# First transformer layer taken one batch at a time, with 64-token expert matmuls and interleaved top-k rounds

## The chip, the core and the metric

The kernel runs on one core of one Trainium2 chip. TensorE (PE) multiplies, VectorE (DVE), ScalarE (ACT) and GpSimd (POOL) work on tiles in on-chip memory, and SyncE (SP) issues most of the transfers. The metric is the device time in microseconds of one execution. Every time below is measured on the chip.

## What is computed

Four batches of 256 tokens with 256 channels pass two gated layers. The reference, cut to its core:

```python
# layer 0: sparse adjacency from ctx, mixed with layernorm(x), then 4 fixed experts
sim = einsum('bhnd,bhmd->bnm', Q, K) / (sqrt(d) * H)          # ctx 4x256x64, H = 4
threshold = top_k(sim, 76)[0][:, :, -1:]
A = sigmoid(sim) * (sim >= threshold); A = (A + A^T) * 0.5
x = x + tanh(g_xattn[0]) * ((1 - gamma) * layernorm(x) + gamma * A)
x4 = layernorm(x).reshape(b, 64, 4, 256)                        # token n goes to expert n % 4
x = x + tanh(g_ffn[0]) * (silu(x4 @ gate) * (x4 @ up)) @ down
# layer 1: masked softmax of scores, then 64 experts, 8 for each token
x = x + tanh(g_xattn[1]) * softmax(scores(ctx) * layernorm(x) + mask)
p = softmax(layernorm(x) @ gate_w); rw = top 8 of p, normed
x = x + tanh(g_ffn[1]) * sum_e rw[:, e] * (silu(g_e) * u_e) @ w_down[e]
```

## The kernel before

Tokens are held as eight tiles of 128 rows, two to a batch. Everything is float32 but for a few counts. Each engine has one hand-written list of work; the lists meet only at semaphores, and each engine takes its list strictly in order. The program falls into three parts.

**The front part** computes layer 0, the attention of layer 1, and the router. Its steps for a batch `b` are these. `keep_top(b)` on DVE finds the 76th largest value of each row of `sim` in ten rounds; a round is two `max` (L991) and two `match_replace` (L995). `transpose_adj(b)` on PE (L573) and `mix_adjacencies(b)` on DVE (L1016, L1020) give the first sum. Each of three layernorms for a batch is `statistics` on DVE (L966 to L972), `inverse_deviation` on POOL (L439, L441), `normalise` on ACT (L827), `transpose_normed` on PE (L583) and `evacuate_xnt` on ACT (L832). The four experts of layer 0 are `expert_gate_up0` (L604) and `expert_down0` (L593) on PE, `silu_and_up0` on ACT (L847, L849) and `up_times_silu` on POOL (L449). They take 128 tokens an expert, out of two batches together, so there are eight calls `q`, four for each half of the batches. Then come `transpose_y0` (L615), `add_layer0` (L1025), `masked_scores`, `exp_scores` and `add_softmax`, `router_logits` on PE (L626), `choose_experts` (L1066 to L1072), `rank_rows` on PE (L672, L673) and DVE's `place_rows` (L1080 to L1092), which ends with `place_at`, the rows at which the batch's tokens are to be put for their experts.

**The placing** is POOL's `place_rows` (L478): 64 indirect transfers from `x_rows` to the DRAM buffer `expert_rows`, sixteen for each batch. The first of each batch waits for that batch's `place_at` and `x_rows`, and for `rows_cleared`, a transfer of 15 MB that fills the buffer with empty rows. SP issues it once, at L349. `inverse_deviation` of later layernorms stands between placements in POOL's list.

**The expert loop** runs over 63 of the 64 experts (and an overflow list). SP loads an expert's rows (L361) only when the placements of all four batches have landed (L360's wait on `placed[b]`); the loop on PE is L704, L715 and L724. Picks are scattered (L499), gathered and summed (L770).

PSUM has eight banks. The list `fills` gives every use of a bank a number in PE's order, and use `i` must wait (`begin(i)`) until use `i - 8` has been copied out. This is told by one semaphore for each copying engine, and `emptied` counts the uses of that engine:

```python
who = fills[i][1]
n = sum(1 for f in fills[:i + 1] if f[1] == who)
eng.wait_ge(evac[who], n)
```

Of the kernel before, what the change touches and what calls it, by code (L numbers as in the profile page):

```python
# [34 lines left out]
def gated_layers_kernel(nc, x, ctx_in, mask_ss, mask_bs, g_xattn, g_ffn, wq0, wk0, gamma_raw, gate_up, down,  # L35
# [12 lines left out]
    TE = HALF // NE0  # L48
# [17 lines left out]
    with ExitStack() as stack:  # L66
# [118 lines left out]
        evac = {who: sem(who + "_evac") for who in ("act", "dve")}  # L185
# [35 lines left out]
        F_CTX, F_PROJ, F_SIM, F_SCORE = {}, {}, {}, {}  # L221
        F_CTX[0] = add_fill("ctx", "act")
# [9 lines left out]
        for b in range(B):  # L232
            F_SCORE[b] = add_fill("score", "act")

        F_ADJT, F_XNT, F_YT, F_XNT2, F_LOGIT = {}, {}, {}, {}, {}
        F_GATE, F_UP, F_DOWN = {}, {}, {}

        def add_gate_up_fills(q):
            F_GATE[q], F_UP[q] = add_fill("gate", "act"), add_fill("up", "act")  # L240

        def add_down_fill(q):
            F_DOWN[q] = add_fill("down", "act")

        for fill, name, who in ((F_ADJT, "adjt", "dve"), (F_XNT, "xnt", "act")):
            for b in (0, 1):
                fill[b] = add_fill(name, who)
        for q in range(NE0):
            if q == NE0 - 1:
                F_ADJT[2] = add_fill("adjt", "dve")  # L250
            add_gate_up_fills(q)
            if q:
                add_down_fill(q - 1)
        add_down_fill(NE0 - 1)
        F_XNT[2] = add_fill("xnt", "act")
        F_ADJT[3] = add_fill("adjt", "dve")
        F_YT[0], F_YT[1] = add_fill("yt", "dve"), add_fill("yt", "dve")
        F_XNT[3] = add_fill("xnt", "act")
        add_gate_up_fills(NE0)
        for q in range(NE0 + 1, 2 * NE0 - 1):  # L260
            add_gate_up_fills(q)
            add_down_fill(q - 1)
        F_XNT2[0], F_XNT2[1] = add_fill("xnt2", "act"), add_fill("xnt2", "act")
        add_gate_up_fills(2 * NE0 - 1)
        F_LOGIT[0], F_LOGIT[1] = add_fill("logit", "act"), add_fill("logit", "act")
        add_down_fill(2 * NE0 - 2)
        add_down_fill(2 * NE0 - 1)
        F_RANK = {}
        F_RANK[0], F_RANK[1] = add_fill("rank", "dve"), add_fill("rank", "dve")
        F_YT[2], F_YT[3] = add_fill("yt", "dve"), add_fill("yt", "dve")  # L270
        F_XNT2[2], F_LOGIT[2] = add_fill("xnt2", "act"), add_fill("logit", "act")
        F_XNT2[3] = add_fill("xnt2", "act")
        F_RANK[2] = add_fill("rank", "dve")
        F_LOGIT[3] = add_fill("logit", "act")
        F_RANK[3] = add_fill("rank", "dve")
# [13 lines left out]
        LAYERNORMS = ((0, None), (1, 0), (1, 1), (1, 2), (1, 3), (2, 0), (2, 1), (3, 0), (3, 1), (2, 2), (2, 3), (3, 2), (3, 3))  # L289
# [11 lines left out]
        def xn_t_view(k, b, permuted):  # L301

            if permuted:
                return xn_t[:, k].rearrange("p (f e b g) -> p f e b g", f=2, e=NE0, b=B // 2)[:, b // 2, :, b % 2, :]
            return xn_t[:, k, b * S:(b + 1) * S]
# [99 lines left out]
        def _(pool):  # L405
# [37 lines left out]
            def up_times_silu(half, experts):  # L443
                for e in experts:
                    q = half * NE0 + e
                    emptied(pool, F_UP[q])
                    if q >= 2:
                        pool.wait_ge(bank_filled, F_DOWN[q - 2] + 1)
# [12 lines left out]
            for n, b in ((1, 2), (1, 3), (2, 0), (2, 1)):  # L461
                inverse_deviation(n, b)
# [28 lines left out]
            for b in range(1, B):  # L491
                place_rows(b, 0, PICKS)
# [784 lines left out]
```

## Time and profile before

| | |
|---|---|
| median of three runs | 417.0 us (415.72 to 417.07) |
| the profiled execution | 417.87 us |
| span of its trace | 416.1 us |
| first placement, last placement | 116.09, 200.86 us |
| first matmul of the expert loop | 206.52 us |

The trace's span leaves out 1.8 us that lie around it. A row of the lists view gives a line, an engine, an operation with output and inputs, the count and the summed and mean time. A row of the time view begins with the start and the duration in us, and ends with the idle time of the engine before it and what ended that.
### The profile page before, as it was taken

The numbers are of one execution on the slowest core, as the hardware profiler recorded it, in microseconds if no ns is written. First come the engines' busy times: TensorE is split into PE (matmuls) and PEld (weight loads), VectorE is DVE, ScalarE is ACT, GpSimd is POOL, SyncE is SP. The second block draws the span as 40 slices with busy tenths as digits, with TensorE's granted clock in tenths as the row PEclk, the third lists the DMA queues.
The fourth block names the chain that finished last, engine by engine and source line by source line (L and its number), as shares of the span: only waits on it lengthen the run. The fifth ranks groups of instructions, "written<-read, shape, count | busy, mean of one in ns | idle before, by whom it ended". The sixth has DMA issues, their size and how long they took to land.

```text
span 416.1 us, 5526 instructions
## 1 busy us (share of the span) xinstructions
PE 275.1 (66%) x1546; PEld 230.9 (55%) x1546; DVE 210.7 (51%) x921; ACT 118.0 (28%) x265; POOL 214.0 (51%) x256
## 2 busy tenths in 40 slices
PE   5898177137801610000199999999999999951997
PEld 1335067037800500000189999889999889931886
DVE  0799999989386679000033433343433343340352
ACT  2264353316634500000023333333333333320000
POOL 2622112013267777777327777777777777771000
PEclk9999999557975555555589999999999999995899
DMA  4899995360013333333498888888888887226891
GB/s 132 312 352 306 318 310 192 91 190 2 1 63 113 126 126 127 126 127 138 148 243 267 273 270 277 271 264 274 261 273 269 269 270 229 74 73 234 325 305 64
DMA packets 47374, 84.12 MB, mean 202 GB/s; under 512 B 10453, under 2 KB 28249, under 8 KB 46320
## 3 DMA queue, kind: packets, MB, share of 16 engines
q1 hardware_dynamic: 38128, 64.87, 49.9%
q0 software_dynamic: 9216, 18.90, 13.0%
q8 instruction: 13, 0.21, 0.2%
q14 instruction: 17, 0.14, 0.1%
HBM read 48.07 MB, written 39.85 MB: 211 GB/s over the span
## 4 chain that ended last, share of the span: by engine, by line
PE 52%; DVE 18%; POOL 16%; issue 7%; DMA 4%; ACT 2%; SPq 1%; POOLq 1%; ACTq 0%
PE psum L715 20%; POOL expert_rows L478 14%; PE psum L724 13%; PE psum L770 7%; PE psum L704 5%; DVE work L995 5%; DVE top L991 5%; DVE stats L966 2%; PE psum L536 2%; PE psum L530 2%; DMA sim<-token_picks 1%; POOL token_picks L499 1%; PE psum L604 1%; DVE adj L1000 1%; DMA gu_w<-expert_rows 1%
## 5 line engine op out<-in xcount | busy, mean ns | idle before, releaser
L499 POOL DMA_INDIRECT token_picks<-down_w,target x126 | 117.3, 931 | 54.9 <-issue 41.1
L715 PE MATMUL psum<-gu_w,wgu 128*96 128x192 f32 x504 | 93.7, 329 | 0.0
L715 PEld LDWEIGHTS psum<-gu_w,wgu 128*96 128x96 f32 x504 | 78.0, 165 | 0.6 <-DVE gu_w L1203 0.2
L478 POOL DMA_INDIRECT expert_rows<-x_rows,place_at x64 | 62.4, 975 | 23.8 <-issue 23.8
L724 PE MATMUL psum<-proj_t,gu_w 96*96 96x256 f32 x252 | 64.8, 379 | 0.0
L927 ACT ACTIVATE gu_w<-psum 96x192 f32<-96x192 f32 x63 | 20.6, 326 | 130.0 <-PE psum L715 130.0
L1208 DVE TENSOR_TENSOR gu_w<-gu_w,psum 96x192 f32<-96x192 f32 x63 | 22.1, 350 | 67.1 <-ACT gu_w L927 67.1
L704 PE MATMUL psum<-ident,gu_w 96*128 96x96 f32 x108 | 14.1, 256 | 53.1 <-DMA gu_w<-expert_rows 53.1
L933 ACT COPY down_w<-psum 96x512 f32<-96x512 f32 x63 | 36.6, 581 | 33.9 <-PE psum L724 33.9
L724 PEld LDWEIGHTS psum<-proj_t,gu_w 96*96 96x96 f32 x252 | 41.1, 163 | 7.1 <-DVE gu_w L1208 0.4
L704 PEld LDWEIGHTS psum<-ident,gu_w 96*128 96x128 f32 x108 | 12.5, 148 | 57.6 <-DMA gu_w<-expert_rows 54.4
L1203 DVE COPY gu_w<-psum 128x384 f32<-128x384 f32 x63 | 34.4, 547 | 0.0
L439 POOL TENSOR_TENSOR rstd<-var_eps,minus_half 128x2 f32<-128x2 f32 (+1 forms) x13 | 10.4, 797 | 46.6 <-DVE var_eps L972 46.5
L1202 DVE COPY target<-gu_w 96x2 uint32<-96x2 uint32 x27 | 4.5, 165 | 52.6 <-PE psum L704 52.6
L991 DVE MAX8 top<-work 128x8 f32<-128x256 f32 x72 | 26.8, 413 | 0.0
L995 DVE MATCH_REPLACE8 work<-top,work 128x256 f32<-128x256 f32 x64 | 25.7, 409 | 0.0
L604 PE MATMUL psum<-xn_t,gu_w 128*128 128x128 f32 x128 | 19.0, 316 | 1.7 <-ACT xn_t L832 1.7
L604 PEld LDWEIGHTS psum<-xn_t,gu_w 128*128 128x128 f32 x128 | 18.4, 231 | 2.4 <-issue 1.3
L449 POOL TENSOR_TENSOR h_t<-silu,up 128x256 f32<-128x256 f32 x8 | 6.1, 762 | 23.9 <-ACT up L849 23.6
L770 PE MATMUL psum<-sim,xn_t 128*128 128x256 f32 x32 | 9.9, 480 | 11.0 <-DMA sim<-token_picks 11.0
L1241 DVE TENSOR_TENSOR xs<-psum,scores 128x256 f32<-128x256 f32 x8 | 3.4, 424 | 27.3 <-PE psum L770 27.3
L583 PE MATMUL psum<-ident,x_rows 128*128 128x128 f32 x16 | 3.4, 351 | 20.8 <-ACT x_rows L827 19.8
(177 smaller groups left out, 397.1 us busy)
## 6 DMA issues: line engine op xcount, KB each, us to landing
expert_rows<-empty_rows SPq DMA_DIRECT2D x1, 15360.0 KB, 69.3
wgu<-in_L_ffn_w_gate_up SPq DMA_DIRECT2D x65, 192.0 KB, 2.9
gu_w<-expert_rows SPq DMA_DIRECT2D x28, 240.0 KB, 4.2
proj_t<-in_L_ffn_w_down SPq DMA_DIRECT2D x65, 96.0 KB, 4.0
sim<-expert_rows SPq DMA_DIRECT2D x18, 240.0 KB, 4.3
work<-expert_rows SPq DMA_DIRECT2D x18, 240.0 KB, 4.2
gu_w<-in_L_ffn_gate_up_proj SPq DMA_DIRECT2D x4, 512.0 KB, 8.2
sim<-token_picks SPq DMA_DIRECT2D x2, 1024.0 KB, 4.9
```

The lines of the kernel that those rows point to most:

```text
L478: pool.indirect_dma_start(rows_dram, bass.IndirectOffsetOnAxis(ap=place_at[:, t, k:k + 1], axis=0), x_rows[:, t, :], None).then_inc(placed ...
L499: pool.indirect_dma_start(picks_dram, bass.IndirectOffsetOnAxis(ap=target[0:SLOTS, e % T_RING, i:i + 1], axis=0), y_slots[0:SLOTS, n, i, : ...
L604: last = pe.matmul(bank(fill)[:, ic * TE:(ic + 1) * TE], gu_w[:, e, k, c:c + P], xn_t[:, k, half * HALF + e * TE:half * HALF + (e + 1) * T ...
L704: last = pe.transpose(psum[:, e % 2, k * CAP + i * SLOTS:k * CAP + (i + 1) * SLOTS], x_slots[n][0:SLOTS, i, k * P:(k + 1) * P], ident[0:SL ...
L715: last = pe.matmul(psum[0:I1, 2 + e % 2, part * CAP:(part + 1) * CAP], wgu[:, n, k, part * I1:(part + 1) * I1], x_slots_t[:, e % 2, k, :], ...
L724: last = pe.matmul(psum[0:SLOTS, 4 + e % 2, i * D:(i + 1) * D], h1_t[:, e % 2, i * SLOTS:(i + 1) * SLOTS], wd[:, n, :], start=True, stop=True)
L770: last = pe.matmul(psum[:, t, 0:D], diag[:, t % 2, k, :], picks[t % K_RING][:, k * D:(k + 1) * D], start=k == 0, stop=k == TOP_K_EXPERTS - 1)
L933: act.copy(y_slots[0:SLOTS, n].rearrange("p i d -> p (i d)"), psum[0:SLOTS, 4 + e % 2, 0:SUBS * D]).then_inc(y_ready, 1)
L991: dve.max(top8[:, t, r], (work if r else sim)[:, t]).then_inc(top8_ready, 1)
L995: dve.match_replace(work[:, t], top8[:, t, r], (work if r else sim)[:, t], REMOVED).then_inc(rest_ready, 1)
L1203: dve.tensor_copy(x_slots_t[:, e % 2].rearrange("p k n -> p (k n)"), psum[:, e % 2, 0:KC * CAP]).then_inc(xt_copied, 1)
L1208: dve.tensor_tensor(h1_t[:, e % 2], silu1[:, e % 2], psum[0:I1, 2 + e % 2, CAP:2 * CAP], ALU.mult).then_inc(h_ready, 1)
```

## The change

The front part is written in another order, and four things in it are of another shape.

1. The four experts of layer 0 take one batch at a time: 64 tokens an expert, sixteen calls `q`. Gate and up share a bank, and four `down` results share one, which ACT empties with two copies. The number of matmuls doubles, each on half the columns.
2. For batches 2 and 3 the product of silu and up moves from POOL to DVE, which reads `up` out of PSUM. ACT then copies no `up`.
3. `keep_top` is cut into pieces of one to ten rounds, and these stand between the layernorm, softmax and router steps of earlier batches.
4. Every kind of bank use has its own semaphore, so ACT and DVE may empty banks in another order than PE fills them. POOL's four groups of sixteen placements stand in batch order as before, but the later layernorms are spread over the first three groups.

SP's list is the same. Its eight weight loads still wait until the last `scores` has been copied, which now comes after batch 0's experts.

The diff, cut:

```diff
-    TE = HALF // NE0
+    TE = S // NE0
...
+        evac = {who: sem(who + "_evac") for who in ("act", "dve", "score", "adjt", "xnt", "yt", "xnt2", "logit", "rank", "gu", "gu_dve", "down")}
+        down_step, silu0_ready = sem("down_step"), sem("silu0_ready")
...
+                  ("gu", 4), ("gu", 5), ("gu", 6), ("gu", 7), ("down", 1),
+                  ("xnt2", 0), ("logit", 0), ("yt", 1), ("adjt", 2), ("rank", 0), ("xnt", 2),
+                  ("gu_dve", 8), ("gu_dve", 9), ("gu_dve", 10), ("gu_dve", 11), ("down", 2),
...
+            def expert_gate_up0(q):
+                b, e = q // NE0, q % NE0
+                begin(F_GU[q])
+                for part in range(2):
                     for ic in range(IC):
                         for k in range(KC):
+                            c, at = part * I0 + ic * P, (part * IC + ic) * TE
+                            last = pe.matmul(bank(F_GU[q])[:, at:at + TE], gu_w[:, e, k, c:c + P],
+                                             xn_t[:, k, b * S + e * TE:b * S + (e + 1) * TE], start=k == 0, stop=k == KC - 1)
+                last.then_inc(bank_filled, 1)
...
+            def evacuate_down(b):
+                filled(F_DOWN[b])
+                for k in range(KC):
+                    last = act.copy(y0_t[:, k, b * S:(b + 1) * S].rearrange("p (n e) -> p e n", e=NE0),
+                                    bank(F_DOWN[b]).rearrange("p (e k n) -> p k e n", k=KC, e=NE0)[:, k])
+                last.then_inc(evac["down"], 1)
...
+            def up_times_silu(*which):
+                for q in which:
+                    dve.wait_ge(silu0_ready, q - 2 * NE0 + 1)
+                    dve.wait_ge(down_step, q - 1)
+                    dve.tensor_tensor(h0_t[:, q % 2].rearrange("p i t -> p (i t)"), silu0[:, q % 2], bank(F_GU[q])[:, IC * TE:2 * IC * TE],
+                                      ALU.mult).then_inc(h0_ready, 1)
```

Three places show the order. A row is a line, an operation with output and inputs, and the output's shape. **PE, experts of layer 0.** Before, the first half of the batches, with the transposes of `adj` for batches 0 and 1 ahead and that for batch 2 in between:

```order
L573 MATMUL psum<-ident,adj 128x128 x8
L583 MATMUL psum<-ident,xn 128x128 x8
L604 MATMUL psum<-xn_t,gu_w 128x128 x16
L593 MATMUL psum<-h_t,down_w 128x128 x4
L604 MATMUL psum<-xn_t,gu_w 128x128 x8
L593 MATMUL psum<-h_t,down_w 128x128 x4
L573 MATMUL psum<-ident,adj 128x128 x4
L604 MATMUL psum<-xn_t,gu_w 128x128 x8
L593 MATMUL psum<-h_t,down_w 128x128 x8
```

After, batch 1 alone, up to its router and the rank of batch 0:

```order
L557 MATMUL psum<-ident,xn 128x128 x4
L584 MATMUL psum<-xn_t,gu_w 128x64 x16
L570 MATMUL psum<-h_t,down_w 128x64 x4
L584 MATMUL psum<-xn_t,gu_w 128x64 x8
L570 MATMUL psum<-h_t,down_w 128x64 x4
L584 MATMUL psum<-xn_t,gu_w 128x64 x8
L570 MATMUL psum<-h_t,down_w 128x64 x8
L557 MATMUL psum<-ident,x_rows 128x128 x4
L606 MATMUL psum<-router,xn_t 128x64 x4
```

One batch now has as many expert matmuls (48) as two batches together had, and its router follows at once. **POOL, placements.** Before, from the first placement on:

```order
L478 DMA expert_rows<-x_rows,place_at 65728x320 x2
L439 TENSOR_TENSOR rstd<-var_eps,minus_half 128x2
L441 TENSOR_TENSOR shift<-neg_mean,rstd 128x2
L478 DMA expert_rows<-x_rows,place_at 65728x320 x2
...
L478 DMA expert_rows<-x_rows,place_at 65728x320 x6
...
L478 DMA expert_rows<-x_rows,place_at 65728x320 x3
...
L478 DMA expert_rows<-x_rows,place_at 65728x320 x51
```

After, with the same pair of layernorm rows at each "...":

```order
L448 DMA expert_rows<-x_rows,place_at 65728x320 x2
L414 TENSOR_TENSOR rstd<-var_eps,minus_half 128x2
L416 TENSOR_TENSOR shift<-neg_mean,rstd 128x2
L448 DMA expert_rows<-x_rows,place_at 65728x320 x7
...
L448 DMA expert_rows<-x_rows,place_at 65728x320 x10
...
L448 DMA expert_rows<-x_rows,place_at 65728x320 x5
...
L448 DMA expert_rows<-x_rows,place_at 65728x320 x9
...
L448 DMA expert_rows<-x_rows,place_at 65728x320 x6
...
L448 DMA expert_rows<-x_rows,place_at 65728x320 x23
```

Seven layernorm pairs stand among the placements now, four did before, and the last stands 23 placements from the end. **DVE, around the first batch's choice.** Before, what follows the last statistics of batch 1:

```order
L1066 MAX l_top<-logits 128x8 x2
L1068 TENSOR_SCALAR l_neg<-l_top 128x2
L1070 MATCH_REPLACE logits_left<-l_top,logits 128x64 x2
L1072 TENSOR_SCALAR chosen<-logits_left 128x128
...
L1080 SCALAR_TENSOR_TENSOR order<-chosen,zeros 128x64 x2
```

After, batch 0's choice comes behind the last round of batch 2, and ahead of the whole search of batch 3:

```order
L1011 MAX top<-work 128x8 x2
L1022 SCALAR_TENSOR_TENSOR adj<-sim,top,adj 128x256 x2
L1099 MAX l_top<-logits 128x8 x2
L1101 TENSOR_SCALAR l_neg<-l_top 128x2
L1103 MATCH_REPLACE logits_left<-l_top,logits 128x64 x2
L1105 TENSOR_SCALAR chosen<-logits_left 128x128
L1038 TENSOR_TENSOR adj<-adj,psum 128x512
L1042 SCALAR_TENSOR_TENSOR xs<-adj,coef,base 128x512
```

All four searches stood ahead of the first choice before.

## Rows read from the trace of the kernel before

**Rows 1.** The page's chain that ended last, by line
```profile
PE psum L715 20%; POOL expert_rows L478 14%; PE psum L724 13%; PE psum L770 7%; PE psum L704 5%; DVE work L995 5%; DVE top L991 5%; DVE stats L966 2%; PE psum L536 2%; PE psum L530 2%; DMA sim<-token_picks 1%; POOL token_picks L499 1%; PE psum L604 1%; DVE adj L1000 1%; DMA gu_w<-expert_rows 1%
```
**Rows 2.** Time view, POOL: first placement, two around a layernorm pair, last ones
```profile
116.09 1.23 POOL L478 DMA_INDIRECT expert_rows<-x_rows,place_at  x1 [5.18 <-issue]
...
121.68 1.02 POOL L478 DMA_INDIRECT expert_rows<-x_rows,place_at  x1 [0.30 <-issue]
...
123.91 1.04 POOL L478 DMA_INDIRECT expert_rows<-x_rows,place_at  x1 [0.16 <-issue]
...
142.46 0.96 POOL L478 DMA_INDIRECT expert_rows<-x_rows,place_at  x1 [0.30 <-issue]
...
200.86 0.96 POOL L478 DMA_INDIRECT expert_rows<-x_rows,place_at  x1 [0.30 <-issue]
```
**Rows 3.** Chain in order of time (start, us, what): the expert loop begins
```profile
206.52 1.72 PE psum L704 x8
```
**Rows 4.** Time view, DVE: the places of batch 3
```profile
146.90 0.39 DVE L1092 TENSOR_SCALAR place_at<-place 128x16 uint32<-128x16 f32 x1
```
**Rows 5.** Chain in order of time: one round of the search on DVE
```profile
54.32 0.65 DVE top L991 x2
54.97 0.79 DVE work L995 x2
```
**Rows 6.** The clearing: the page's DMA issues (KB, us to landing), then its issue
```profile
expert_rows<-empty_rows SPq DMA_DIRECT2D x1, 15360.0 KB, 69.3
...
16.19 0.61 SPq L349 DMA_DIRECT2D expert_rows<-empty_rows  x1
```
**Rows 7.** Stretches, PE's L604 (128 columns), then L626 (64), L770 (256)
```profile
94.06:98.06 4.00, 4.00 (x19) 0.50 0.02 6
...
135.50:137.20 1.70, 1.70 (x8) 0.50 0.47 172
109.53:111.27 1.74, 1.74 (x16) 1.00 0.00 0
...
390.00:398.00 8.00, 8.00 (x38) 1.00 0.88 279
```
**Rows 8.** Chain in order of time: sixteen records of L604 at the full clock
```profile
107.91 1.79 PE psum L604 x16
```
**Rows 9.** Stretches, all of PE, before and at changes of the granted clock
```profile
32.70:39.70 7.00, 7.00 (x16) 1.00 1.00 308
...
97.00:98.00 1.00, 1.00 (x6) 0.50 0.00 0
98.00:99.00 1.00, 1.00 (x10) 0.90 0.00 0
...
383.00:388.00 5.00, 4.97 (x12) 0.50 1.01 426
```
**Rows 10.** Time view, DVE: layer 0 added with its statistics, and masked scores
```profile
117.00 0.75 DVE L1025 SCALAR_TENSOR_TENSOR xs<-psum,tg,xs 128x512 f32<-128x512 f32 x1
...
118.93 0.16 DVE L972 TENSOR_SCALAR var_eps<-mv 128x2 f32<-128x2 f32 x1
...
121.00 0.88 DVE L1034 SCALAR_TENSOR_TENSOR work<-xs,mv,scores 128x256 f32<-128x256 f32 x2
...
122.72 0.24 DVE L1042 SCALAR_TENSOR_TENSOR exp_bias<-row_max,rstd 128x1 f32<-128x1 f32 x2
```
**Rows 11.** Time view: batch 2 from its last statistics to its router
```profile
132.23 0.20 DVE L972 TENSOR_SCALAR var_eps<-mv 128x2 f32<-128x2 f32 x1
...
132.44 1.09 ACT L827 ACTIVATE x_rows<-xs,shift,rstd 128x256 f32<-128x256 f32 x2 [4.09 <-POOL shift L441]
134.80 0.65 ACT L832 COPY xn_t<-psum 128x256 f32<-128x256 f32 x2 [1.27 <-PE psum L583]
...
133.68 1.08 PE L583 MATMUL psum<-ident,x_rows 128*128 128x128 f32 x4 [18.61 <-ACT x_rows L827]
135.50 1.97 PE L626 MATMUL psum<-router,xn_t 128*128 128x64 f32 x8 [0.74 <-ACT xn_t L832]
```

More of the change, by code:

```diff
@@ L248, in gated_layers_kernel @@
[L248 to L262, printed above, removed]
@@ L563, in _ @@
                     emptied(pe, F_PROJ[w, half])
-            for b in range(B):
-                query_times_key(1, F_SCORE, b)
             def transpose_adj(b):
@@ L859, in copy_logits @@
                 filled(F_LOGIT[b])
[L860 removed]
+                act.copy(logits[:, span(b)].rearrange("p h n -> p (h n)"), bank(F_LOGIT[b])[:, 0:HB * NE]).then_inc(evac["logit"], 1)
             def exp_logits(b):
@@ new lines, in _ @@
+            sigmoids(1)
+            scale_x(0)
+            copy_scaled(scores, F_SCORE, 0, SCORE_SCALE)
+            copy_scaled(scores, F_SCORE, 1, SCORE_SCALE)
+            normalise(1, 0)
+            evacuate_xnt(F_XNT, True, 0)
+            sigmoids(2)
+            sigmoids(3)
+            act.preload_act_table(ACT.Silu)
+            copy_scaled(scores, F_SCORE, 2, SCORE_SCALE)
+            scale_x(1)
+            silu_and_up0(0, 1, 2, 3)
+            normalise(1, 1)
+            evacuate_down(0)
@@ L882, in _ @@
+            copy_scaled(scores, F_SCORE, 3, SCORE_SCALE)
+            evacuate_xnt(F_XNT, True, 1)
+            silu_and_up0(4, 5)
             act.preload_act_table(ACT.Exp)
-            for b in (2, 3):
-                normalise(1, b)
-                evacuate_xnt(F_XNT, True, b)
             exp_scores(0)
+            act.preload_act_table(ACT.Silu)
+            silu_and_up0(6, 7)
+            scale_x(2)
+            evacuate_down(1)
+            normalise(3, 0)
+            evacuate_xnt(F_XNT2, False, 0)
@@ L980, in _, with keep_top @@
                               ALU.mult).then_inc(evac["dve"], 1)
-            def keep_top(b):
+            def keep_top(b, first, end):
                 emptied(dve, F_SIM[b])
                 tiles = range(b * HB, (b + 1) * HB)
-                for r in range(ROUNDS):
+                for r in range(first, end):
                     for t in tiles:
@@ L1125, in _ @@
+            up_times_silu(8)
+            keep_top(3, 1, 2)
+            up_times_silu(9)
+            softmax_and_statistics(1)
+            keep_top(3, 2, 3)
+            up_times_silu(10)
+            keep_top(3, 3, 4)
+            up_times_silu(11)
+            keep_top(3, 4, 6)
+            choose_experts(1)
+            keep_top(3, 6, 7)
+            place_rows(1)
+            keep_top(3, 7, ROUNDS)
+            add_layer0(2)
             mix_adjacencies(3)
             statistics(1, 3)
-            for b in (0, 1):
-                add_layer0(b)
-                statistics(2, b)
```

376 lines of the change are left out of this document (198 added, 178 removed).

## The prediction

> **What bounds the kernel now.** I read the chain that ended last first [rows 1]: most of it is PE's loop over the experts (L704, L715, L724) and the last sums (L770), and 14% is POOL's placing (L478). Next POOL in time: the first placement starts at 116.09, the last at 200.86, and from 142.46 on it goes 46 steps without a gap [rows 2]: (200.86 - 142.46) / 46 = 1.27 us each. The loop begins at 206.52 [rows 3], 5.66 after the last placement starts: landing, and SP's load of the first rows. Batch 3's places were ready at about 147.3 [rows 4], long before POOL reached them. So DVE's front part ends 35 us too early to matter at its end; what decides is when POOL may start and whether it ever waits. From 206.52 to the span's end is 209.6 us, in which nothing changes. The whole sum is therefore one number: **when does the last placement start?** It has two bounds. POOL: first placement plus 64 x 1.27, plus layernorm pairs at 2.23 - 1.27 = 0.96 each [rows 2]. Data: the last batch's places plus 15 x 1.27 = 19.1.
>
> **The change, part by part.**
>
> *What moves earlier.* Batch 0's choice now comes after three searches, not four, and without batch 1's steps. A round of the search takes 0.65 + 0.79 = 1.44 [rows 5], a search about 14.6, ten rounds. On the other side the clearing of the row buffer lands at 16.19 + 69.3 = 85.5 [rows 6], and before that nothing may be placed. SP's order is unchanged, so I keep 85.5. If everything else were ready, the first placement would gain 116.1 - 85.5 = 30.6 us, and three more pairs cost 2.9 of that: a gain of at most 27.7.
>
> *What it costs on PE.* The matmuls of layer 0's experts double in number at half the columns. Is a 64-column matmul cheaper? At the lower clock a record of 128 columns (L604) takes 4.00 / 19 = 0.21, and one of 64 columns (the router, L626) 1.70 / 8 = 0.2125 [rows 7]; at the full clock 1.79 / 16 = 0.112 [rows 8] and 1.74 / 16 = 0.109. Both come with a 128x128 weight load. So halving the columns saves nothing, and a batch's 48 matmuls are 96 records: **20.4 us at the lower clock, 10.5 at the full one**. Before, two batches together paid that.
>
> *Which clock.* This decides the sign. The granted column says 1.00 for 32.70 to 39.70, but sixteen records of 256 columns took 7.00 there, 0.44 each, in matmuls of 64 rows [rows 9]; the last sums, 128 rows and also 256 columns, take 8.00 / 38 = 0.21 at the full clock [rows 7] and 4.97 / 12 = 0.41 at 0.50 [rows 9]. So the early stretch really ran at 1.2 GHz, and an unbroken run of half-height matmuls did not change that. What PE did before it rose to 2.4 GHz was each time a stretch of full-height matmuls of 128 columns (98 us) or 256 (after 388 us) [rows 7, 9]. After the change no such stretch is left ahead of the expert loop: scores are half height, expert matmuls half as wide, the rest is transposes and routers. The full-clock row with 64 columns [rows 7] follows at once on 128-column matmuls, so it shows that the clock can stay, not that it would rise. I take 1.2 GHz for the whole front part.
> The Trainium skill speaks against this: "TensorE: Matmul & The Clock Gate", Part 1, says that activity over time releases the throttle, whatever the number of matmuls; by that rule each batch's long run would reach 2.4 GHz, and the sum would be that of the first rival below. The half-height run does not agree with it. The same page, Part 4, adds that transposes do not count as activity, which no row here tests alone.
>
> *Layout and small terms.* DVE gets eight products of 128x128 from PSUM, under 0.5 each: two 128x256 steps take 0.88 together (L1034) [rows 10]; POOL loses eight of 0.7. Bank semaphores by class cost nothing by themselves. Four more table loads on ACT stand nearly all where ACT waits for PE.
>
> *The sum at 1.2 GHz.* I laid the five lists beside each other, every step starting when its engine and its inputs are free. The same laying of the old lists gives 116.7 for the first and 201.6 for the last placement, against 116.1 and 200.9, so I compare with 201.6. Landmarks:
> - Batch 0 is normalised at 41, its experts run from 43.6 to 65.1 (20.4, and batch 1's transposes of `adj` in between). Then scores 3 (two matmuls of 256 columns, 1.9), two times four transposes (0.9 each), ACT's copy 0.7: batch 1's experts run from 69.7 to 90.3.
> - The router of batch 0 is *behind* batch 1's experts on PE. From 90.3: copies and layernorm 1.8, transposes 1.1, copy 0.65, router 1.97 [rows 11], copy: DVE gets logits at 96.1 and has by then waited for them, and for transposes before. Choice 1.2, mix and statistics of batch 2 2.8, places 2.1: first placement at **102.4**, 17 after the clearing, 14 earlier than before.
> - Batch 2's experts from 104.5 to 125.2, its clock-bound path again before batch 1's router; places of batch 1 at **133.8**. POOL has finished group 0 at 127.3 and waits.
> - The last three rounds of batch 3's search (4.3), layer 0 of batch 2, mix, statistics: 142.2. Batch 3's experts start at 146.3; with router and transposes between, the ranks of batch 2 come at 168.9, its places at **170.1**. POOL had ended group 1 at 161.6 and waits 8.5.
> - Layer 0 of batch 3 is added at 172.5, statistics and masked scores follow with 2.0 and 1.9 [rows 10], softmax and statistics to 181.7. The layernorm pair stands behind nine placements of group 2 and starts at 183.2. From there as in [rows 11]: 1.0, 1.1, 1.1, 0.65, 1.97, with hops and a copy 189.4; choice and places 3.6: **193.0**, exactly when POOL has done group 2 (170.1 + 16 placements + two pairs + 0.7 of waiting).
> - Last placement at 193.0 + 19.0 = 212.0, against 201.6: **+10.4 us**. From the profiled 417.87: 428.3. That execution lay 0.9 above the median, so I predict **427.5**.
> Bounds: at 0.205 a record the last placement is at 209.3, at 0.23 (a record's price if starts after waits cost more) at 218.7, so 424.5 to 434; I take 0.2125, the 64-column row itself.
>
> **Rivals.**
> 1. *The clock rises in each batch's run*, as for 128 columns. The same laying with 0.11 a record once a run has lasted as long as the one at 94 us needed: experts of batch 0 from 43.5 to 56.4, of batch 1 60.1 to 71.8; places of batch 0 at 82.2. Now the clearing binds: first placement 85.5, and DVE waits 3.3 for a layernorm that stands behind two placements. Places of batches 1, 2 and 3 at 108.8, 139.2 and 161.3, POOL free at 161.4: last placement at 180.3, **-21.3**, that is 395.7. For it: PE would be busy for more than 10 us on end. Against: [rows 9] as read above.
> 2. *The clock rises in some of the four runs only.* The two layings differ by 31.7, about 8 a batch: 404, 412 or 420.
> 3. *The clearing lands later*, held up by nothing now but perhaps by the weight loads' new time: at 95 instead of 85.5 the fast case loses 9.5 (405), the slow case nothing.
> 4. *The placing stays where it was*, because the data bound of batch 3 cancels what the start gains: the two meet if a record costs 0.183, between the two prices; then 417. It needs a clock that changes midway.
>
> **How the numbers follow.** Slow clock throughout: 0.57, 424.5 to 434. Rival 1: 0.32, 393 to 400. Rivals 2 and 3: 0.09, nearly all of it faster. Rival 4: 0.02. A measurement tells 0.3% (1.3 us) from no change. Faster 0.40, same 0.02, slower 0.58. No range on one side holds 8 in 10, so it runs from 394 to 433; the likeliest case's own is 424.5 to 434.
>
> **What would show it.** Right: granted clock 0.50 (or 64-column records at 0.21) from the first expert matmul to past the placing; first placement near 102; POOL waiting before groups 1 and 2, 6 and 8 us; DVE idle for logits; last placement near 211; loop start 5.7 later, and 209.6 from there. Wrong on the clock: records at 0.11 and first placement at 85.5. Wrong on the price: records clearly under 0.21 at 0.50, so that halving the columns did save. Wrong on the tail: anything but 209.6 after the loop's start.

## The result, and the profile after

The changed kernel takes **430.81 us** (430.04 to 432.85, 4 runs), the kernel before, beside it on the same chip, 416.72 us (415.72 to 417.07). The ratio is 1.035, with a 95% interval of 1.0308 to 1.0392: 14.1 us slower. The forecast was 427.5, with 424.5 to 434 for its own case and 394 to 433 over all cases.

First the page, its chain by line and two lines of the busy tenths (40 slices of 10.7 us):

```profile
PE psum L719 19%; PE psum L728 13%; PE psum L584 11%; POOL expert_rows L448 7%; PE psum L774 7%; PE psum L570 6%; PE psum L708 5%; DVE work L1015 3%; DVE top L1011 2%; PE psum L557 2%; PE psum L513 1%; DVE stats L987 1%; PE psum L606 1%; DMA sim<-token_picks 1%; POOL rstd L414 1%
...
PE   4896999974993399222039999999999999980997
POOL 2713011013772572677714777777777777772000
```

Before, layer 0's expert matmuls (L604) were 1% of this chain and the placing 14% [rows 1]. Now L584 and L570, the same work in 64-column pieces, are 17%, and the placing is 7%: half of POOL's share has gone, and PE's experts have taken its place.

POOL in time shows the same with its waits. The columns are start, duration, engine, line, operation, tiles, and in brackets the idle time ahead of it:

```profile
104.29 1.23 POOL L448 DMA_INDIRECT expert_rows<-x_rows,place_at  x1 [1.76 <-issue]
...
136.17 0.96 POOL L448 DMA_INDIRECT expert_rows<-x_rows,place_at  x1 [7.65 <-issue]
...
144.10 0.72 POOL L414 TENSOR_TENSOR rstd<-var_eps,minus_half 128x2 f32<-128x2 f32 x1 [4.45 <-DVE var_eps L993]
...
172.83 0.96 POOL L448 DMA_INDIRECT expert_rows<-x_rows,place_at  x1 [9.25 <-issue]
...
196.54 0.96 POOL L448 DMA_INDIRECT expert_rows<-x_rows,place_at  x1 [0.94 <-issue]
...
215.88 0.96 POOL L448 DMA_INDIRECT expert_rows<-x_rows,place_at  x1 [0.30 <-issue]
```

The first placement starts 11.8 us earlier than in [rows 2] (104.29 against 116.09), and the last one 15.0 us later (215.88 against 200.86). In between POOL waits 7.65, 4.45 and 9.25 us for the next batch's data; before, it went 46 steps without a gap. The loop over the experts follows at 221.43, 5.55 after the last placement, and the rest of the span is 428.3 - 221.43 = 206.9.

Why the data come late is seen on PE. Time view of PE, the first batch's experts, then stretches (duration, PE busy, number of records, granted clock, DMA share, GB/s):

```profile
43.77 7.09 PE L584 MATMUL psum<-xn_t,gu_w 128*128 128x64 f32 x32
50.65 1.92 PE L570 MATMUL psum<-h_t,down_w 128*128 128x64 f32 x8
...
70.09:77.09 7.00, 7.00 (x32) 1.00 0.30 84
...
221.43:225.27 3.84, 3.84 (x15) 1.00 0.97 268
225.27:227.00 1.73, 1.73 (x15) 1.00 1.06 278
...
389.10:399.35 10.25, 3.07 (x7) 0.50 0.72 273
```

32 records take 7.00 us, 0.219 each. That is the price of the lower level, 1.2 GHz, as [rows 7] have it for 64 columns, and not the 0.109 of the full clock. The granted column nevertheless reads 1.00, as it did in [rows 9] for a stretch that ran at the lower level: in these traces the column shows no level below 1.00 until the clock falls for the first time, so ahead of that the records' own durations have to be read. By them the first rise lies at 225.27, 3.84 us into the loop over the experts: 15 records take 3.84 us up to there and the next 15 take 1.73. Ahead of it no run of matmuls in the front part is faster than the lower level, where the kernel before reached the full level in both of its expert runs.

### The profile page after: what moved, and what is told of

It is laid out like the page before. It is cut to its first block, busy times and chain, and to the rows that moved or that the text cites. A ratio compares the mean times of both kernels' runs of the same rounds, so it can differ in the third digit from the quotient of the medians.

```text
span 428.3 us, 5963 instructions
## 1 busy us (share of the span) xinstructions
PE 335.4 (78%) x1738; PEld 289.9 (68%) x1738; DVE 214.1 (50%) x929; ACT 123.0 (29%) x269; POOL 209.5 (49%) x256
## 4 chain that ended last, share of the span: by engine, by line
PE 69%; DVE 10%; POOL 9%; issue 4%; DMA 3%; ACT 2%; SPq 1%; POOLq 0%; PEldq 0%; DVEq 0%; ACTq 0%
PE psum L719 19%; PE psum L728 13%; PE psum L584 11%; POOL expert_rows L448 7%; PE psum L774 7%; PE psum L570 6%; PE psum L708 5%; DVE work L1015 3%; DVE top L1011 2%; PE psum L557 2%; PE psum L513 1%; DVE stats L987 1%; PE psum L606 1%; DMA sim<-token_picks 1%; POOL rstd L414 1%
## 5 line engine op out<-in xcount | busy, mean ns | idle before, releaser
L476 POOL DMA_INDIRECT token_picks<-down_w,target x126 | 115.4, 916 | 54.5 <-issue 41.1
L584 PE MATMUL psum<-xn_t,gu_w 128*128 128x64 f32 x256 | 57.1, 421 | 2.2 <-ACT xn_t L831 2.2
L584 PEld LDWEIGHTS psum<-xn_t,gu_w 128*128 128x128 f32 x256 | 55.9, 332 | 4.1 <-ACT xn_t L831 3.4
L570 PE MATMUL psum<-h_t,down_w 128*128 128x64 f32 x128 | 30.1, 422 | 0.0
L414 POOL TENSOR_TENSOR rstd<-var_eps,minus_half 128x2 f32<-128x2 f32 (+1 forms) x13 | 10.4, 797 | 38.8 <-DVE var_eps L993 38.6
L570 PEld LDWEIGHTS psum<-h_t,down_w 128*128 128x128 f32 x128 | 28.8, 333 | 0.0
L422 POOL TENSOR_TENSOR h_t<-silu,up 128x128 f32<-128x128 f32 x8 | 3.6, 453 | 36.5 <-ACT up L847 36.5
L845 ACT ACTIVATE silu<-psum 128x128 f32<-128x128 f32 x16 | 4.4, 277 | 46.0 <-PE psum L584 46.0
L557 PE MATMUL psum<-ident,x_rows 128*128 128x128 f32 x16 | 4.4, 428 | 15.9 <-ACT x_rows L826 15.6
```

The source lines that it names most:

```text
L476: pool.indirect_dma_start(picks_dram, bass.IndirectOffsetOnAxis(ap=target[0:SLOTS, e % T_RING, i:i + 1], axis=0), y_slots[0:SLOTS, n, i, : ...
L570: last = pe.matmul(bank(i)[:, c:c + TE], down_w[:, e, ic, hc * P:(hc + 1) * P], h0_t[:, q % 2, ic, :], start=ic == 0, stop=ic == IC - 1)
L584: last = pe.matmul(bank(F_GU[q])[:, at:at + TE], gu_w[:, e, k, c:c + P], xn_t[:, k, b * S + e * TE:b * S + (e + 1) * TE], start=k == 0, st ...
```

## The experiments

Each was timed beside the kernel before. For e1 to e8 that one took 416.7 to 417.1 us; for e9 to e12 it took 477 to 478, of which more below. "Last placement" is the start of the last of POOL's 64 placements, the one number of the prediction's sum. A matmul with f32 operands shows as two records.

### Is it the clock, and what decides it?

**e3_old_split**, the old order with the new matmuls:

```
-  for k in range(KC):
-      last = pe.matmul(bank(fill)[:, ic*TE:(ic+1)*TE], gu_w[...], xn_t[..., 128 columns])
+  for g in (0, TE // 2):
+      for k in range(KC):
+          last = pe.matmul(bank(fill)[:, ic*TE+g:ic*TE+g+64], gu_w[...], xn_t[..., 64 columns from g])
   (the down matmuls likewise)
```

> Edit: the kernel before, in its own order, with each expert matmul of layer 0 (128 columns) issued as two of 64 columns into the two halves of the same region: twice as many matmuls, as in the change, and nothing else changed. Theory: no clock rise ahead of the expert loop any more, records at 0.2135 throughout; the five lists laid beside each other give the last placement 46.6 us later (two batches' 192 records stand in one run, twice), so 463 us (450 to 468). Rival A in the form that doubling alone costs and the clock rises as before: 8.4 us more, 425 us.

Measured: 460.34 us (459.72 to 460.92), ratio 1.1054 (1.1035 to 1.1072). One stretch of all of PE, and POOL's last placement:

```profile
57.23:98.88 41.65, 41.65 (x196) 1.00 0.49 152
...
245.66 0.96 POOL L478 DMA_INDIRECT expert_rows<-x_rows,place_at  x1 [0.30 <-issue]
```

PE is busy for 41.65 us without a gap, in full-height matmuls (192 records of 64 columns and four transposes), and 196 records take 0.2125 each: the lower level from end to end (the 1.00 is again the column ahead of the first fall). In the three executions that were not profiled the column's mean is 0.825 to 0.829 instead of 0.989, at the same time within 1.2 us; their traces were not kept, and it is one more reason not to read the level from that column. So here being busy didn't raise the clock, and neither did full height alone. The Trainium skill, "TensorE: Matmul & The Clock Gate", Part 1, has sustained activity release the throttle; taken as "PE busy", that rule doesn't hold for this row.

**e5_old_twice**, as many matmuls, but 128 columns each:

```
-  for k in range(KC):
+  for k in list(range(KC)) * 2:
       last = pe.matmul(... 128 columns ..., start=k == 0, stop=k == KC - 1)
   (the down matmuls likewise)
```

> Edit: the kernel before, in its own order, with each expert matmul of layer 0 issued twice at its full 128 columns (the second contraction writes over the first), so as many matmul instructions as e3_old_split, and 128 columns instead of 64. The pair tells the number of matmuls from the clock. Theory (columns decide the clock): it rises about 4 us into each run as in the kernel before, records at 0.11 from there, last placement 11.5 us later than before: 428 us (425 to 434). Rival A (number of matmuls is the price): as e3_old_split, 460 us.

Measured: 430.24 us (430.06 to 431.08), ratio 1.0309. PE's first expert run, then the last placement:

```profile
57.01 9.72 PE L604 MATMUL psum<-xn_t,gu_w 128*128 128x128 f32 x64 [0.93 <-ACT xn_t L832]
...
68.35 3.74 PE L604 MATMUL psum<-xn_t,gu_w 128*128 128x128 f32 x32
...
214.11 0.96 POOL L478 DMA_INDIRECT expert_rows<-x_rows,place_at  x1 [0.30 <-issue]
```

64 records in 9.72 us, then 32 in 3.74 (0.117 each): the clock rose in the first run. e3 and e5 have the same order and the same number of matmuls; they differ by **30.1 us**, and by 31.55 in the last placement, and that is the columns, through the clock. Rival A, that the number is the price whatever is streamed, falls. What number alone costs is e5 less the kernel before, 13.1 us against the one timed beside it (417.12) and 13.5 against 416.72.

**e1_wide**, the changed kernel with 128-column gate/up matmuls:

```
-  last = pe.matmul(bank(F_GU[q])[:, at:at + TE], gu_w[...], xn_t[:, k, own 64 columns])
+  last = pe.matmul(bank(F_GU[q])[:, at:at + 2*TE], gu_w[...], xn_t[:, k, the pair's 128 columns])
   (ACT and DVE read the expert's own half of each 128)
```

> Theory (the front part stays at 1.2 GHz because no stretch of full-height matmuls of 128 or more columns is left in it). Edit: in the changed kernel each gate/up matmul of layer 0's experts streams the 128 columns of an expert pair instead of its own 64; ACT and DVE read only the expert's own half of the bank. Same number of matmuls, same order, same results; only 8 of 12 matmuls of an expert are wider. The theory expects the clock to rise within about 4 us of batch 0's first expert matmul, records at 0.11 from there, first placement at the clearing's landing, about 85.5, last placement near 180: 215.88 of the changed kernel minus 35.6, so 395 us (range 393 to 401). Rival A (the number of matmuls is the price, whatever they stream): nothing changes in records at 0.2135, last placement 215.9, 431 us. Rival B (the order of the lists, with routers and layernorms behind experts and placements, holds the placing back): first placement stays above 100 though the clock rises; 415 to 425 us.

Measured: **405.67 us** (404.25 to 407.45), ratio 0.9751 (0.9711 to 0.9791): streaming twice the columns, half of which nobody reads, makes the changed kernel 25.1 us faster, and faster than the kernel before by 11.0. The gate/up run at the head of batches 0 to 3, then POOL's groups:

```profile
43.75 5.10 PE L592 MATMUL psum<-xn_t,gu_w 128*128 128x128 f32 x32
...
60.72 3.84 PE L592 MATMUL psum<-xn_t,gu_w 128*128 128x128 f32 x32 [0.74 <-ACT xn_t L839]
...
86.94 5.67 PE L592 MATMUL psum<-xn_t,gu_w 128*128 128x128 f32 x32 [0.74 <-ACT xn_t L839]
...
125.94 6.60 PE L592 MATMUL psum<-xn_t,gu_w 128*128 128x128 f32 x32 [0.74 <-ACT xn_t L839]
...
85.59 1.24 POOL L455 DMA_INDIRECT expert_rows<-x_rows,place_at  x1 [1.75 <-issue]
113.93 0.95 POOL L455 DMA_INDIRECT expert_rows<-x_rows,place_at  x1 [5.52 <-issue]
146.34 0.96 POOL L455 DMA_INDIRECT expert_rows<-x_rows,place_at  x1 [5.03 <-issue]
188.61 0.96 POOL L455 DMA_INDIRECT expert_rows<-x_rows,place_at  x1 [0.30 <-issue]
```

The first placement is where the theory had it, 85.59, though not by the clearing alone: that landed at 83.9, and DVE wrote the places at 84.6. The last came 8.6 us later than its 180, and the 405.67 us lie outside the 393 to 401 that were expected: batch 1 enters its experts at the full level (3.84 for 32 records), but batches 2 and 3 pay 5.67 and 6.60. The clock had fallen earlier, in or right behind a wait of PE of 2.26 us (at about 73.7, ahead of the transposes of x_rows, and at about 101.1), and in the 5.0 and 5.3 us of idle time ahead of the experts nothing raised it. The expectation had let it stay up. Rival B, that the lists' order holds the placing at 100 or more, falls.

**e4_half**, half of the matmuls at the lower clock:

```
-  for k in range(KC):  ... start=k == 0, stop=k == KC - 1
+  for k in range(1):   ... start=True, stop=True
   (ic in the down matmuls likewise)
```

> Edit: the changed kernel with half of layer 0's expert matmuls left out (one half of each contraction, k = 0 and ic = 0 alone), so 48 records of 64 columns a batch; the output differs by what they would add. Theory: clock still low (64 columns), but the records' time halves to 10.2 a batch; last placement 183.9 in the laying, so 399 us (395 to 405). If order (rival B) were the limit: 415 or more. If the clock rises here: 394, which the records' duration (0.21 or 0.11) tells apart.

Measured: 401.5 us (400.19 to 403.23). PE's first expert run, and POOL's first and last placement:

```profile
43.77 3.67 PE L584 MATMUL psum<-xn_t,gu_w 128*128 128x64 f32 x16
...
85.29 1.23 POOL L448 DMA_INDIRECT expert_rows<-x_rows,place_at  x1 [1.76 <-DMA expert_rows<-empty_rows]
...
184.94 0.96 POOL L448 DMA_INDIRECT expert_rows<-x_rows,place_at  x1 [0.31 <-issue]
```

16 records in 3.67: the lower clock, half the records, and the kernel is 29.3 us faster than the changed one. PE's time in layer 0's experts falls by 4 x 10.2 = 40.8 us and the last placement comes 30.9 earlier, so three quarters of that time were on the path that ends last. e1 saves about as much by the clock (27.3 at the last placement) as e4 by number. The clearing landed at 84.3 here and DVE wrote the places at 84.3 too; below 85.3 little is to be had at that end.

### Can the clock be raised from outside?

**e2_burst**: 24 dummy matmuls ahead of each batch's experts.

```
+  def keep_busy(q, times):
+      begin(F_GU[q])
+      for _ in range(times):
+          pe.matmul(bank(F_GU[q])[:, 0:P], ident[:], ctx_rows[:, 0:2, :], start=True, stop=True)
+  keep_busy(0, 24)                      (and 4, 8, 12 ahead of the later batches)
   emptied(pe, F_XNT[0])
   expert_gate_up0(0)
```

> Edit: in the changed kernel 24 matmuls of 128x128 by 128 columns, f32 and full height, that write over a bank about to be filled, stand ahead of each batch's expert matmuls of layer 0; the experts stay at 64 columns. Results unchanged. Question: can the clock be raised from outside, and does a run of 64-column matmuls hold it? If it rises in each burst and is held: a burst costs 4.4 us at the lower clock, the records behind it 0.11; first placement 88, last 187, so 402 us. If it rises and falls again within the run: between, 425 to 445 us. If it never rises: each burst is 5 us of delay on the way of its batch, last placement at 234, 449 us.

Measured: 423.99 us (419.5 to 425.19), ratio 1.0141.

```profile
43.88 7.32 PE L626 MATMUL psum<-ctx_rows,ident 128*128 128x128 f32 x48
51.03 3.68 PE L584 MATMUL psum<-xn_t,gu_w 128*128 128x64 f32 x32
...
72.57 3.68 PE L584 MATMUL psum<-xn_t,gu_w 128*128 128x64 f32 x32
```

I had priced the burst wrongly, as 24 records; it is 48, and took 7.32, 6.20, 7.62 and 8.01 us in the four batches, each on the path: 29.2 us instead of 17.6. That is only part of the miss of 22 us against the 402 of a held clock; the last placement came at 206.09 instead of 187, and in batch 2 the level was lost again in a wait of 2.26 us for `h0`. But one answer is clear: the 64-column records behind the burst cost 0.115 to 0.12, in all of batches 0 and 1. Matmuls that had not raised the clock ran at it, and four bursts that compute nothing make the kernel 6.8 us faster than the changed one.

**e8_narrow_idle** put such dummies only where PE stood idle anyway:

```
+  keep_busy(F_XNT[2], 11)
   transpose_normed(F_XNT, xn, xn_ready, 2)
+  keep_busy(F_XNT[3], 12)
   transpose_normed(F_XNT, xn, xn_ready, 3)
```

> Edit: the changed kernel with its 64-column expert matmuls, and only the fill of PE's idle time ahead of the transposes of xn of batches 2 and 3 (11 and 12 dummy matmuls of 128 columns). Theory: 64-column matmuls can't raise the clock but hold it, as they did for a whole batch behind each burst of e2_burst. Then batches 0 and 1 stay at 0.21 a record, batches 2 and 3 run at 0.11 throughout: first placement unchanged at 104.3, last at 200 instead of 215.9: 415 us (412 to 421). If the clock does not rise in the idle fill or is lost at once: 431 to 432.

Measured: 428.5 us (428.26 to 430.4): 2.3 below the changed kernel instead of 16. PE in batch 2:

```profile
98.60 3.72 PE L626 MATMUL psum<-ctx_rows,ident 128*128 128x128 f32 x22
103.75 0.63 PE L557 MATMUL psum<-ident,xn 128*128 128x128 f32 x4 [1.43 <-ACT xn L833]
105.12 4.88 PE L584 MATMUL psum<-xn_t,gu_w 128*128 128x64 f32 x32 [0.74 <-ACT xn_t L838]
...
111.67 3.62 PE L584 MATMUL psum<-xn_t,gu_w 128*128 128x64 f32 x16
```

The fill did raise the clock (four transposes in 0.63 instead of 1.09), and it was lost inside the first 32 expert records (4.88), back to 3.62 for 16. The expectation that 64 columns hold the clock was wrong here, though in e2 they had held it for whole batches. In batch 3 of this trace they held it through their first 32 records (3.79), and it fell in the 3.60 us in which PE then waited for `h0`.

**e6_wide_idle** is e1 with the same two fills:

> Edit: e1_wide, and in the idle time of PE ahead of the transposes of xn of batches 2 and 3 (5.0 and 5.3 us idle there in e1_wide) 11 and 12 dummy matmuls of 128x128 by 128 columns (22 and 24 records, 4.9 and 5.3 us at 1.2 GHz) into the bank that these transposes then fill. Theory: PE's own idle time lets the clock fall, and e1_wide enters the experts of batches 2 and 3 at 0.50; with the idle time filled they run at 0.11 a record from the first, places of batches 1, 2 and 3 come 4.5, 6.3 and 6.3 us earlier, last placement near 182.3: 399.5 us (397 to 403). Rival: the clock does not rise in so short a fill, or falls again in the 0.7 us ahead of the experts: 405.7 as e1_wide, or up to 1 us more.

Measured: 405.88 us (401.58 to 406.95), the rival's time and not the theory's 399.5, but not by the rival's cause. PE in batches 2 and 3, and two stretches of PE there:

```profile
88.78 3.84 PE L592 MATMUL psum<-xn_t,gu_w 128*128 128x128 f32 x32 [0.74 <-ACT xn_t L846]
...
126.05 3.84 PE L592 MATMUL psum<-xn_t,gu_w 128*128 128x128 f32 x32 [0.74 <-ACT xn_t L846]
133.42 1.94 PE L577 MATMUL psum<-h_t,down_w 128*128 128x64 f32 x8 [3.54 <-DVE h_t L1071]
...
129.90:133.42 3.52, 0.00 (x0) 0.97 0.39 141
133.42:140.10 6.68, 6.44 (x30) 0.50 0.31 112
```

Both fills worked: 32 records in 3.84 at the head of both batches. But batch 3's down matmuls wait 3.54 for `h0` from DVE, whose multiplication stands behind the softmax and statistics of batch 2; what PE gained it waits out, and in that wait the clock falls to 0.50 again. Besides, batch 1's run had already lost the clock in this execution (first placement 87.89 instead of 85.59), with a program that up to there is that of e1: 128-column matmuls lose it at times too.

**e7_wide_idle_pool** moves three of POOL's layernorm pairs: (2, batch 2) and (3, batch 3) one placement earlier each, and (3, batch 2) two. (In the changed kernel's list of placements under "The change", two placements stand between the ten and the five, with one more pair: the groups are 2, 7, 10, 2, 5, 9, 6 and 23, 64 in all with seven pairs.)

> Edit: e6_wide_idle, and on POOL the layernorm pair of (2, batch 2) one placement earlier, the one of (3, batch 3) one earlier. What is left of the order's price: DVE waits 3.2 us for the pair (2, 2) behind placements in e1_wide. Laying the lists gives 1.3 us less than e6_wide_idle: 398 us (396 to 402). Rival: the placing is bound elsewhere and nothing changes (within 0.5 us of e6_wide_idle).

Measured: **402.87 us** (398.38 to 404.72), ratio 0.962 (0.9569 to 0.9671), the fastest of all, but outside the 396 to 402 expected, and neither the theory's 1.3 below e6_wide_idle nor the rival's nothing. The last placements of the two profiled executions, 189.14 and 189.64, lie only 0.5 apart, and the loops start 0.7 apart. Another 1.6 of the 2.4 us between these two executions lies behind the loop's start, where nothing in the program differs. So what moving the pairs is worth is not shown beyond half a microsecond, and in e1's trace, without any fill, the last placement lay at 188.61.

### What stays open: the other idle time, and the old order

**e9_wide_filled**, **e12_filled_again** (the same kernel) and **e10_narrow_filled** fill nearly all idle time around the experts:

```
   expert_gate_up0(13)
+  keep_busy(F_XNT2[2], 14)
   expert_down0(12)
   ...
+  keep_busy(F_GU[4], 3)                 (and ahead of y0's transposes, and in batch 2)
   emptied(pe, F_XNT[1])
```

> Edit: e7_wide_idle_pool with the rest of PE's idle time around the experts filled by dummy matmuls too: 3 ahead of the transposes of y0, 3 in each wait for ACT's copy of xn (0.74 us), 7 and 3 among batch 2's last experts (waits of 1.6 and 0.8 us in e6_wide_idle), 14 ahead of batch 3's first down matmuls (3.5 us there, in which the clock fell to 0.50 again). Theory: in e6_wide_idle the gain went because PE's waits for h0 let the clock fall within the batches; filled, it stays at 1.00 from batch 2's transposes to its router, and through batch 3's experts; places of batch 2 at about 138 instead of 147.6, last placement near 181: 397 us (394 to 401). Rival: the clock isn't what holds batch 2's places back, but DVE's and ACT's lists; 402 to 404 as e7_wide_idle_pool.

> Edit: the same fills, the changed POOL order and 10 dummies ahead of batch 0's experts, but the experts at the changed kernel's own 64 columns. Two runs stand against each other: behind the long bursts of e2_burst 64-column matmuls ran at 0.11 for whole batches, in e8_narrow_idle the clock fell 2.7 us into batch 2's. If 64 columns hold the clock once no idle time is left: as e9_wide_filled within 2 us. If they don't hold it behind a short fill: it falls within each batch, records at 0.21 from there, first placement at 92 to 100, 410 to 428 us.

> Edit: none against e9_wide_filled, the same kernel once more. There the kernel before took 477 us instead of 417 (its expert loop was longer), and in batch 2 of the filled kernel ACT stood 5.5 us in a wait put down to nothing on this core, so e9 does not tell whether the fills help. Where the kernel before takes 417: group 1's places then come about 5.5 us earlier than the 119.2 of e9, the last placement at 184 to 188 instead of 196.8; against 189.1 of e7_wide_idle_pool that is 400 us (396 to 403) if the held clock is worth anything beyond e7; if it is not, 402 to 404 as e7.

Measured: 465.6 us (e9), 467.53 (e10) and 467.76 (e12), where the kernel before took 477.4 beside the first two and 477.93 beside the third: ratios 0.9749 (0.9702 to 0.9795), 0.9761 (0.9713 to 0.9809) and 0.9836 (0.9782 to 0.989). On these chips engines stood still at many places for a few us with no releaser on this core, in the loop above all, which took 218.6 us in e9 and 164.8 in e7. One such row, ACT in batch 2 of e9; then PE's granted clock from batch 2's fill on:

```profile
102.12 0.28 ACT L867 ACTIVATE silu<-psum 128x128 f32<-128x128 f32 x1 [5.51 <-remote]
...
84.00:98.00 14.00, 11.96 (x101) 1.00 0.69 223
129.40:137.00 7.60, 7.53 (x65) 1.00 0.30 109
137.00:146.00 9.00, 8.40 (x75) 1.00 0.29 106
```

The fills do most of what they are for: batch 3's experts run at 1.00 up to their last down matmuls (1.97 for 8 records, behind waits of 2.3 and 1.5 us). In batch 2 the level fell at about 100.7 all the same. Whether that beats e7 is **not settled**: such stops put group 1's places of e9 at 119.21 against 115.8 in e7, and e12 met the same conditions instead of answering. Against the kernel before beside them e9 and e12 gain 11.8 and 10.2 us, e7 14.3. e10 says something about 64 columns all the same:

```profile
48.27:70.00 21.73, 21.30 (x178) 1.00 0.86 287
86.00:96.00 10.00, 8.09 (x68) 0.99 0.54 177
98.00:104.00 6.00, 6.00 (x30) 0.50 0.30 109
```

Behind ten dummies 178 records, about 150 of them of 64 columns, ran through batches 0 and 1 in 21.30 us (0.12 each) with the clock held; in batch 2 it was lost some 2 us after a wait of 1 us for `h0`; in batch 3 it held again. The time, 1.9 us above e9's, lies within the 2 us that were expected for a held clock, so the time doesn't tell the two cases apart. So 64-column matmuls hold the clock sometimes (e2, e10 in batches 0, 1 and 3) and sometimes not (e8 and e10 in batch 2). Both losses came soon after PE had stood idle for about a microsecond or more. With 128 columns batch 2 kept the clock behind the very wait at which e10 lost it (0.98 us in e6, 0.97 in e9), which points at the columns; but e6 lost it in its batch 1 behind waits of 0.9 and 0.7 us. With one trace of each this stays an observation.

**e11_old_idle** gives the kernel before the same care:

> Edit: the kernel before, in its own order and with its own matmuls, with PE's idle time ahead of both expert runs of layer 0 filled with dummy matmuls (9, 4 and 3 ahead of the first, 7 and 3 ahead of the second). Question: is the gain of the filled versions the clock alone, or the new order that the clock makes worth having? Expected from the laying: the experts of both halves start at 1.00 and save 2 us each, but the first placement waits for DVE's four searches, so 416 us (413 to 417.5). If the clock alone were the gain: 405 or less.

Measured: 479.22 us (474.12 to 481.12), ratio 1.0024 (0.9992 to 1.0055).

```profile
56.60 3.81 PE L604 MATMUL psum<-xn_t,gu_w 128*128 128x128 f32 x32 [0.27 <-ACT xn_t L842]
...
118.17 1.23 POOL L478 DMA_INDIRECT expert_rows<-x_rows,place_at  x1 [5.17 <-issue]
```

The expert run starts at the full level, and the first placement is no earlier than in [rows 2]. In the old order the clock isn't worth having sooner: the ratio leaves room for 0.1% at most. That DVE's four searches are what holds it back is the reading that the expectation started from, and the unmoved first placement agrees with it.

## Why the prediction was right, and where it was off

**The three parts of the 14.1 us**, each from a pair of runs:

| step | from | to | us |
|---|---|---|---|
| twice the matmuls, clock still rises | before, 416.7 | e5, 430.2 | +13.5 |
| 64 columns, clock never rises | e5, 430.2 | e3, 460.3 | +30.1 |
| the new order and all else of the change | e3, 460.3 | after, 430.8 | -29.5 |

The new order is worth 29.5 us at the same matmuls and the same clock; the way in which it cuts the matmuls costs 43.6. With a clock that rises the order is worth 24.6: e5, 430.24, against e1, 405.67, which have the same number of matmuls (e1's down matmuls have 64 columns).

**Which clock: right, and it decided the sign.** The prediction read from [rows 9] that a busy half-height stretch had not raised the clock, and concluded that with the 128-column stretches gone nothing would. No rise came before 225.27. The row that it argued from was of another shape (64 rows, 256 columns), so the step to full-height matmuls of 64 columns was a leap, given 0.57; e3 is what bears it out. Its list of the rises left one out: in the kernel before the clock also rose at 210.8, 4.3 us into the loop, behind matmuls of 96 and 192 columns (L704, L715), and the same place is the first rise of the changed kernel. Rival 1, whose time was 395.7, is what e1 would have been had the clock also stayed up between batches; its laying gave first placement 85.5 (e1: 85.59) and last placement 180.3 (188.61).

**The price of a record: right.** Batch 0's experts were laid from 43.6 to 65.1 and lay from 43.77 to 65.3; batch 1's 69.7 to 90.3, measured 70.09 to 90.8. Halving the columns saved nothing.

**The landmarks: right in order, late by a growing bit.** First placement 102.4 laid, 104.29 measured; POOL's wait ahead of group 1 about 6, measured 7.65; ahead of group 2 8.5, measured 9.25; batch 3's experts 146.3 against 148.19; the third pair of batch 3 183.2 against 185.81; the last group 193.0 against 196.54; last placement 212.0 against 215.88. **The step that was mis-sized is the handing over from engine to engine.** DVE's writes of the places of batches 0 and 3, to set beside POOL's starts at 104.29 and 196.54:

```profile
103.17 0.17 DVE L1125 TENSOR_SCALAR place_at<-place 128x16 uint32<-128x16 f32 x1
...
195.59 0.17 DVE L1125 TENSOR_SCALAR place_at<-place 128x16 uint32<-128x16 f32 x1
```

The last placement is 3.9 late, in three pieces. The places of batch 3 end at 195.76 where 193.0 was laid: 2.8 had piled up ahead of POOL. PE's expert runs themselves took what was laid (21.5, 20.7 and 20.7 us for batches 0 to 2), so it lies between them; one piece that can be named is the layernorm behind batch 1's experts, 2.2 us of waiting on PE where 1.8 was laid. POOL then starts 0.8 after the write, 0.95 in batch 0, and the landmarks had nothing for that, as if places ready meant placement started. The last fifteen placements took 19.34 instead of 19.0. The laying of the old lists, by which I corrected, was late by 0.7, so a constant correction taken from it had the wrong sign. Together it makes 4.6 us: +15.0 instead of +10.4.

**The tail: wrong by 2.7**, in the other direction: 206.9 behind the loop's first matmul instead of 209.6. Nothing in the code differs there. The first matmuls of the last sums, before and after:

```profile
383.03 6.31 PE L770 MATMUL psum<-sim,xn_t 128*128 128x256 f32 x16 [11.04 <-DMA sim<-token_picks]
...
396.28 5.21 PE L774 MATMUL psum<-sim,xn_t 128*128 128x256 f32 x16 [10.18 <-DMA sim<-token_picks]
```

Of the 2.7, 0.9 is the wait for the gathered picks, 1.1 are these 16 records, of which fewer ran at the lower level, and 0.8 lies in the loop, at whose start the lower level lasted 3.84 us instead of 4.3. "Nothing changes from there" held for the instructions and not for the transfers and the clock. Nor is it peculiar to the change: in the profiled executions of e1 to e8 the same stretch took 206.8 to 211.8 us. A tail taken from one execution carries an error of that size, and that it went the helpful way is luck.

The two misses have opposite signs, 4.6 and 2.7, so the profiled execution came out only 1.7 above the 428.3 forecast for it. The other 1.6 of the 3.3 between the medians is where the profiled executions lie: 0.9 above the median before, 0.8 below it after. So the nearness of the forecast owes something to errors that cancelled.

**The bound of the clearing** was not reached, as said for the slow case. The transfer landed at 84.5 (laid 85.5). In e1 and e4 the first placements, at 85.6 and 85.3, come when the clearing (83.9, 84.3) and the places (84.6, 84.3) are ready within 0.7 us of each other.

The sign "last placement near 211" among those of being right does not fit the prediction's own sum, 212.0; measured 215.88.

## What to carry to other kernels

Before a matmul is cut into narrower ones, look at which stretches of the trace raised TensorE's clock and whether the cut leaves one standing; here halving the columns saved no time per record and cost 30 us of clock beside 13.5 us of doubled count. A reordering that is good can be hidden by such a loss: the order gained 29.5, and streaming columns that nobody reads, in the same number of matmuls, brought the gain out. And where a laying of lists is corrected by what it gives for the kernel before, count the handovers between engines in each: a start behind another engine's last write carries a piece (0.8 to 0.95 us for POOL here) that a row of work without gaps doesn't show.

## What the runs showed of the hardware that I had not expected

- 41.65 us of unbroken full-height f32 matmuls, nearly all of 64 columns (196 records at 0.2125), left the clock at 1.2 GHz (e3); in the same place 128 columns raised it within the first 64 records (e5: 9.72 us for all of them, 3.74 for the next 32).
- Dummy matmuls in idle time raise it as well: 22 records of 128 columns, and the transposes 1.4 us later took 0.63 instead of 1.09 (e8).
- 64-column matmuls ran at the full level for whole batches in some runs and lost it within 32 records in others (e2 and e10 against e8).
- The granted column can read 1.00 for 225 us in which every run of matmuls took the lower level's time.
- The same kernel's executions differ by 1.3 to 1.6%, and the fastest have the highest mean granted clock: e6 from 401.58 (0.889) to 406.95 (0.869), e7 from 398.38 (0.888) to 404.72 (0.869), where the kernel before on that chip stayed within 416.24 to 419.97.
- On two other chips the kernel before took 477.4 and 477.9 us instead of 416.7 to 417.1, and the traces of e9 to e12 there show short stops put down to "issue" or "remote", such as the 5.51 us of ACT shown above. Why is open.
